# Flamingo-style gated decoder: layer 2's keys, queries and values of all batches projected in its setup and kept in DRAM scratch

## The reference

```python
x = x + tanh(g_xattn[0]) * L0_xattn(layernorm(x), ctx, ctx)     # layer 1
x = x + tanh(g_ffn[0])   * L0_ffn(layernorm(x), ...)
x = x + tanh(g_xattn[1]) * L1_xattn(layernorm(x), ctx, mask, ...)  # layer 2
x = x + tanh(g_ffn[1])   * L1_ffn(layernorm(x), W1, W2)

# L1_xattn: 16 heads of 32 columns
q = w8a8_linear(x, wq, bq)            # rows and weights rounded to whole numbers of 8 bits
k = cond @ wk.T + bk
v = cond @ wv.T + bv
attn = softmax(q @ k.T / sqrt(32) + mask)
return w8a8_linear(attn @ v, wo, bo)

# L1_ffn: W1 and W2 rounded to -1, 0, 1; rows rounded to whole numbers
return bitlinear(silu(bitlinear(x, W1)), W2)
```

## Time and profile before

| | us |
|---|---|
| median of 3 runs | 1078.93 |
| lowest, highest | 1077.7, 1079.21 |
| profiled execution | 1081.88 |
| its span in the profile | 1080.1 |

### The profile page before, as it was taken

One profiled execution on the slowest core, in us unless ns is written; L12 is line 12 of the kernel. 1 busy time (PEld: TensorE's weight loads), 2 busy tenths in 40 slices (PEclk: granted clock), 3 DMA queues, 4 the chain that ended last, 5 costly groups with the idle time before them and its releaser, 6 DMA issues.

```text
span 1080.1 us, 16123 instructions
## 1 busy us (share of the span) xinstructions
PE 938.5 (87%) x5776; PEld 621.2 (58%) x5784; DVE 743.1 (69%) x1925; ACT 555.1 (51%) x1104; POOL 72.6 (7%) x53
## 2 busy tenths in 40 slices
PE   3999879999999977569989889998989998899567
PEld 2777767767767654356644456644566544566333
DVE  5887863361626058479978688786699796799564
ACT  3444412221212137358854679845689647689243
POOL 4444100000000000000010000010000010000100
PEclk9999989999999998879999999999999999999869
DMA  6331400010203066861017820019420149300001
GB/s 214 117 117 39 156 1 1 32 48 1 78 1 117 1 214 237 192 156 41 2 39 157 195 78 2 4 53 208 128 79 2 40 86 197 108 2 2 1 0 40
DMA packets 45888, 85.99 MB, mean 80 GB/s; under 512 B 7409, under 2 KB 7409, under 8 KB 44785
## 3 DMA queue, kind: packets, MB, share of 16 engines
q1 hardware_dynamic: 42448, 80.24, 26.9%
q0 software_dynamic: 576, 4.19, 1.1%
q10 hardware_dynamic: 2784, 0.54, 0.3%
HBM read 43.01 MB, written 8.39 MB: 48 GB/s over the span
## 4 chain that ended last, share of the span: by engine, by line
PE 33%; DVE 10%; SPq 6%; issue 6%; DMA 5%; ACT 4%; POOL 0%; POOLq 0%; DVEq 0%; ACTq 0%
PE psum L1309 7%; PE psum L1326 6%; PE psum L1284 5%; PE psum L1382 5%; PE psum L1352 5%; SPq L962 5%; DMA k<-k_lo 4%; ACT probs L1110 2%; PE psum L1251 1%; PE psum L1368 1%; DVE amax L1531 1%; SPq L973 1%; DVE probsT L1619 1%; DVE xn L1699 1%; PE psum L1335 1%
## 5 line engine op out<-in xcount | busy, mean ns | idle before, releaser
L1110 ACT ACTIVATE probs<-psum,neg_max 128x512 f32<-128x512 f32 x256 | 174.8, 692 | 32.1 <-DVE neg_max L1593 32.0
L1593 DVE CUSTOM_DVE_ANT_0 psum<-psum,m_in 128x512 f32<-128x512 f32 x256 | 174.0, 702 | 18.5 <-issue 18.5
L1309 PE MATMUL psum<-ident,probs 128*128 128x128 f32 x1024 | 154.0, 274 | 0.0
L1309 PEld LDWEIGHTS psum<-ident,probs 128*128 128x128 f32 x1024 | 127.4, 141 | 21.0 <-issue 3.3
L1284 PE MATMUL psum<-k,q 128*128 128x512 f32 x256 | 125.9, 497 | 13.4 <-ACT probs L1110 8.3
L505 PE MATMUL psum<-w_sb,hT 128*128 128x512 f32 x256 | 115.1, 593 | 0.0
L389 ACT ACTIVATE hT<-psum,b_col 128x256 f32<-128x256 f32 x64 | 26.8, 470 | 136.2 <-PE psum L425 136.2
L1619 DVE COPY probsT<-psum 128x512 f32<-128x512 f32 x128 | 87.7, 685 | 2.6 <-PE psum L1309 2.3
L423 PE MATMUL psum<-xselT_hi,w_hi 128*128 128x256 f32 x256 | 82.8, 323 | 4.2 <-ACT onehotT L383 4.2
L1101 ACT COPY probsT<-psum 128x512 f32<-128x512 f32 x128 | 75.1, 587 | 19.8 <-PE psum L1309 19.8
L945 POOL TENSOR_TENSOR xres<-xres,xn 128x512 f32<-128x512 f32 x16 | 19.9, 1274 | 876.4 <-DVE xn L1699 876.4
(11 more groups left out here) (207 smaller groups left out, 1685.5 us busy)
## 6 DMA issues: line engine op xcount, KB each, us to landing
c_in<-in_ctx_dram SPq DMA_DIRECT2D x8, 1024.0 KB, 5.4
bw_in<-in_L_ffn_W_dram SPq DMA_DIRECT2D x8, 1024.0 KB, 11.2
k<-k_hi SPq DMA_DIRECT2D x32, 256.0 KB, 6.8
k<-k_lo SPq DMA_DIRECT2D x32, 256.0 KB, 8.5
q<-q_hi SPq DMA_DIRECT2D x64, 128.0 KB, 2.7
q<-q_lo SPq DMA_DIRECT2D x64, 128.0 KB, 2.4
xres<-in_x_dram SPq DMA_DIRECT2D x4, 1024.0 KB, 5.3
w_raw<-in_L_ffn_w_dram POOLq DMA_DIRECT2D x4, 1024.0 KB, 5.1
```

The lines of the kernel that those rows point to most:

```text
L1110: act.activation(probs[:, u % 4, :], psum[u % SCORE_BANKS][:, :], ACT.Exp, scale=-1.0, bias=neg_max[:, u:u + 1], accum_out=prob_sum[:, nt, ...
L1309: mm = pe.transpose(turn_bank(u)[:, l * P:(l + 1) * P], probs[:, u % 4, l * P:(l + 1) * P], ident[:, :])
L1593: dve.tensor_tensor_reduce(bank[:, :], bank[:, :], m_in[:, nt, :], -1.0, LOWEST, ALU.add, ALU.min, neg_max[:, u:u + 1]).then_inc(masked_re ...
```

## The change

Layer 2's setup makes the keys, queries and values of all four batches (`project`, on PE, ACT and DVE, with all three queues written so that batch b+1's context is turned between batch b's value tiles). SP writes them to DRAM scratch (`k_dram`, `q_dram`, `v_dram`) between its loads. The attention of batch b loads `k4`, `q4` (16 transfers of 256 KB each, into 32 partitions, four per group of four heads) and `vv` from there; group g of batch b+1 is loaded once batch b's scores of group g are made. The tails lose their projections.

Other parts of the edit:

- Keys and values: weights and context are split into a high half and the rest, and a product is three matmuls in a single pass each (`three`) instead of one in float32. DVE makes the low halves. Two banks serve the keys and two the values, so tile 2 waits for the eviction of tile 0.
- Both feed-forward weights pass through one input buffer `bw_in` in the place of `k4`; the first is turned in batch 1's projection and the second in batch 3's. ACT rounds all chunks, DVE clips them.
- The queries' rows of x are loaded into `xn` and worked on in place; `x_in` for batch 0 is the last of the initial loads.
- The value products of a half group are spread over four steps instead of two (`i % 2 == 0`).

```diff
+    k_dram = nc.dram_tensor("k_dram", (B, 2, C, S), F32, kind="Internal").ap()
+    q_dram = nc.dram_tensor("q_dram", (B, 2, C, S), F32, kind="Internal").ap()
+    v_dram = nc.dram_tensor("v_dram", (B, S, C), F32, kind="Internal").ap()
...
+        bw2T = at("bw2T", [P, FT, C], FP8, bw2T_at)
...
+        c_in = at("c_in2", [P, T, C], F32, x_at)
+        ctxT = [[at(f"ctxT{s}{i}", [P, CT_, S], F32R, q4_at + 16 * K * s + 8 * K * i) for i in range(2)] for s in range(2)]
+        k_hi = at("k_hi", [P, CT_, S], F32R, kst_at)
+        k_lo = at("k_lo", [P, CT_, S], F32R, kst_at + 8 * K)
+        q_hi = at("q_hi", [P, CT_, S], F32R, xres_at)
+        q_lo = at("q_lo", [P, CT_, S], F32R, probs_at)
+        q_raw = at("q_raw", [P, CT_, S], F32, probs_at)
+        v_out = [m_in, m_in, m_in, xn]
         BWC = FT * C // 4
-        bw_in = [at("bw_in0", [P, 4, BWC], F32, k4_at), at("bw_in1", [P, 4, BWC], F32, q4_at)]
-        bw_whole = [at(f"bw_whole{k}", [P, BWC], BF16, (xres_at, probs_at)[k // 2] + 4 * K * (k % 2)) for k in range(4)]
-        magnitudes = [at(f"magnitudes{k}", [P, BWC], BF16, m_at + 4 * K * k) for k in range(2)]
+        bw_in = at("bw_in", [P, 4, BWC], F32, k4_at)
...
+                def load_keys(b, g):
+                    for i, part in enumerate((0, 1, 0, 1)):
+                        sp.dma_start(k4[HD * i:HD * (i + 1), HPG * g:HPG * (g + 1), :].bitcast(F32),
+                                     k_dram[b, part, P * g:P * (g + 1), :].rearrange("(r d) s -> d r s", d=HD)
+                                     ).then_inc(k4_loaded[g], 16)
...
+                def save_keys(b):
                     sp.wait_ge(k_hi_ready, b * CT_ + CT_)
                     sp.wait_ge(k_lo_ready, b * CT_ + CT_)
-                    for g, part in enumerate((k_hi, k_lo, k_hi, k_lo)):
-                        for r in range(HPG):
-                            sp.dma_start(k4[HD * g:HD * (g + 1), r::HPG, :].bitcast(F32),
-                                         part[HD * r:HD * (r + 1), :, :].bitcast(F32)).then_inc(k_stacked, 16)
-
-                def stack_queries(b, q_hi, q_lo):
-
-                    for half in range(2):
-                        sp.wait_ge(q_hi_ready, b * CT_ + 2 * half + 2)
-                        sp.wait_ge(q_lo_ready, b * CT_ + 2 * half + 2)
-                        for g, part in enumerate((q_hi, q_hi, q_lo, q_lo)):
-                            for r in range(HPG):
-                                heads = slice(2 * half * HPG + r, 2 * (half + 1) * HPG, HPG)
-                                sp.dma_start(q4[HD * g:HD * (g + 1), heads, :].bitcast(F32),
-                                             part[HD * r:HD * (r + 1), 2 * half:2 * half + 2, :].bitcast(F32)
-                                             ).then_inc(q_stacked[half], 16)
-
+                    for i, part in enumerate((k_hi, k_lo)):
+                        sp.dma_start(k_dram[b, i].rearrange("(c p) s -> p c s", p=P),
+                                       part[:, :, :].bitcast(F32)).then_inc(k_saved, 16)
...
                 sp.wait_ge(sh.x2_stored, 16 * B)
-                sp.wait_ge(magnitude_ready, 7)
+                for b in range(B):
+                    if b + 1 < B:
+                        sp.wait_ge(qxT_psum, 2 * b + 2)
+                        load_rows(b + 1)
+                    save_keys(b)
+                    if b == 1:
+                        for k in range(4):
+                            sp.wait_ge(bwT_psum, 2 * k + 2)
+                            sp.dma_start(bw_in[:, k, :], bw2[P * k:P * (k + 1), :]).then_inc(bw_loaded[1][k], 16)
+                    save_queries(b)
+                    if b + 2 < B:
+                        sp.wait_ge(ctxT_psum, (b + 2) * CT_)
+                        load_context(b + 2)
+                    if b + 1 < B:
+                        save_values(b)
+                sp.wait_ge(v_saved, 3 * 16)
                 sp.dma_start(m_in[:, :, :], rows(mask, 0)).then_inc(m_loaded, 16)
...
+                sp.dma_start(vv[:, :, :], rows(v_dram, 0)).then_inc(vv_loaded, 16)
+                sp.wait_ge(k_saved, 32)
+                sp.wait_ge(q_saved, 32)
+                sp.wait_ge(bwT_psum, 16)
+                for g in range(GROUPS):
+                    load_keys(0, g)
+                    if g < 2:
+                        load_queries(0, g)
+                save_values(B - 1)
+                for g in range(2, GROUPS):
+                    load_queries(0, g)
+                sp.dma_start(x_in[:, :, :], rows(x_mid, 0)).then_inc(x_loaded, 16)
+
+                for b in range(B):
+                    if b + 1 < B:
+                        sp.wait_ge(x_used, b * T + T)
+                        sp.dma_start(x_in[:, :, :], rows(x_mid, b + 1)).then_inc(x_loaded, 16)
+                        for g in range(GROUPS):
+                            sp.wait_ge(score_psum, b * UNITS + GU * (g + 1))
+                            sp.wait_ge(k_saved, 32 * (b + 2))
+                            sp.wait_ge(q_saved, 32 * (b + 2))
+                            load_keys(b + 1, g)
+                            load_queries(b + 1, g)
+                        sp.wait_ge(masked_ready, (b + 1) * UNITS)
+                        sp.dma_start(m_in[:, :, :], rows(mask, b + 1)).then_inc(m_loaded, 16)
+                        sp.wait_ge(av_psum, (b + 1) * HG)
+                        sp.wait_ge(v_saved, 16 * (b + 2))
+                        sp.dma_start(vv[:, :, :], rows(v_dram, b + 1)).then_inc(vv_loaded, 16)
...
+                def project(b):
+                    normed_queries(b)
+                    key_highs(b, range(2))
+                    if b == 0:
+                        magnitude(0, 0)
+                    rounded_queries(b)
+                    key_highs(b, range(2, 3))
+                    query_scales(b)
+                    turned_rows(b, (2, 3))
+                    key_highs(b, range(3, CT_))
+                    if b % 2 == 0:
+                        for k in range(1 if b == 0 else 0, 4):
+                            magnitude(b // 2, k)
+                    query_highs(b)
+                    if b % 2:
+                        turned_bw(b // 2)
+                    if b + 1 < B:
+                        turned_context(b + 1, range(CT_))
+                    if b % 2 == 0:
+                        round_chunks(b // 2)
...
+                def three(dst, left, right, start, stop):
+
+                    (l_hi, l_lo), (r_hi, r_lo) = left, right
+                    pe.matmul(dst, l_hi, r_hi, start=start, stop=False)
+                    pe.matmul(dst, l_hi, r_lo, start=False, stop=False)
+                    return pe.matmul(dst, l_lo, r_hi, start=False, stop=stop)
...
+                def keys(b, tiles):
+                    for o in tiles:
+                        if o >= 2:
+                            pe.wait_ge(k_lo_ready, b * CT_ + o - 1)
+                        for c in range(CT_):
+                            if o == 0:
+                                pe.wait_ge(ctxT_lo_ready, b * CT_ + c + 1)
+                            mm = three(psum[o % 2][:, :], [p[:, c, o * P:(o + 1) * P] for p in wkT],
+                                       [p[:, c, :] for p in ctxT[b % 2]], c == 0, c == CT_ - 1)
+                        mm.then_inc(k_psum, 1)
+
+                def values(b, t):
+                    if t >= 2:
+                        pe.wait_ge(v_ready, b * T + t - 1)
+                    else:
+                        pe.wait_ge(q_scaled, b * CT_ + t + 1)
                     for c in range(CT_):
-                        for t in range(CT_):
-                            mm = pe.transpose(psum_b[4 * i + c][:, t * P:(t + 1) * P], w_whole[:, i, t, c * P:(c + 1) * P],
-                                              ident_b[:, :])
-                        mm.then_inc(linear_psum, 1)
-                for i, (w, ready) in enumerate(((wk_in, linear_act_ready), (wv_in, linear_dve_ready))):
+                        mm = three(psum[2 + t % 2][:, :], [p[:, c, t * P:(t + 1) * P] for p in ctxT[b % 2]],
+                                   [p[:, c, :] for p in wvT], c == 0, c == CT_ - 1)
+                    mm.then_inc(v_psum, 1)
...
+                def project(b):
+
+                    if b:
+                        pe.wait_ge(q_scaled, b * CT_)
+                    keys(b, range(3))
+                    query_rows(b)
+                    keys(b, range(3, CT_))
+                    queries(b)
+                    if b % 2:
+                        turn_bw(b // 2)
+                    for t in range(T):
+                        values(b, t)
+                        if b + 1 < B:
+                            context(b + 1, (t,))
+                    if b % 2 == 0:
+                        pe.wait_ge(sxrow_ready, b + 1)
+                        bw_sums(b // 2)
...
+                        if 0 <= hg < HG and i % 2 == 0:
+                            l = i // 2
...
+                pe.wait_ge(v_ready, B * T)
```

(31 more changed lines are left out.)

## The result

The kernel after takes 1192.75 us (median of 4 runs, 1191.26 to 1194.8), the kernel before 1078.32 beside it. The ratio is 1.1067, 95% interval 1.1038 to 1.1095: slower, 5.8 us above the forecast 1187 and inside its range. The profiled execution has a span of 1192.7 us, 112.6 more than before.

What follows compares the result with a forecast made beforehand. PE was busy 87% of the span, attention bound by a mix of DVE, ACT and PE. First score +130.4, x_in +25.5, batches -39.7, value products -8.0: +108.2 on 1081.9, 1190.1, less 3.0 to the median: 1187, range 1125 to 1225.

Steps and rivals of the forecast that it cites:

- first score: Layer 2's setup: with four projections ahead of it, PE's first attention score moves from 471.2 to 601.6 us, +130.4.
- stall for x_in: Batch 0's ninth attention step: DVE waits for x_in, last in SP's load queue, landing at 637 but due at 611.5, +25.5.
- batches: Tails of three batches lose their projections, each worth 13.2 us by comparing batch 0 with batch 3: -39.7 us.
- value products: Attention: spreading them over four steps instead of two uses DVE's gap per half group; 8 us gained taken.
- The bound below: Attention: low end of the gain allowed for spreading value products, between 0 and 22 us.
- R0: Setup: moment DVE finishes the root for batch 0, put at 413.8 us, 24.7 after the setup's start.
- even batches: Setup: from DVE's finished root in an even batch to the next batch's root, 39.7 us.
- the odd one: Setup: from DVE's finished root in batch 1 to the next, with weight rounding and turning, 56 us.
- last R to first score: End of setup: from DVE's finished root for batch 3 (R3, 549.2) to the first score (601.6), 52.4 us.
- rival C: Setup: PE sets the pace, values end at 539.5 and the first score comes at 547; 1133 us, chance 0.15.
- Rival D: Setup: further waits of the same kind, say 8 us in each projection, +32; 1219 us, chance 0.20.
- Rival E: Batch tails: next attention could run into the tail, so batches gain far more, deciding from 3 x 49 us; chance 0.01.

Runs made afterwards that it cites:

- x_in early: Kernel after, with only SP's load of batch 0's x_in moved to when the last context is turned, not behind k4 and q4: 1172.63 us.
- without projections: Kernel before, with batches 1 to 3 making no context, keys, values, queries or stacking and scoring against batch 0's: 1036.73 us.
- one product: Kernel after, with each keys and values product in layer 2 one matmul (high half by high half) instead of three: 1171.76 us.
- the query highs: Kernel after, with ACT making the queries' high halves ahead of the magnitudes in batches 0 and 2: 1189.31 us.
- the rounding: Kernel after, with ACT's rounding of the feed-forward weight chunks moved into gaps in batches 1 and 3: 1186.42 us.
- the turned banks: Kernel after, with DVE turning the weight banks before making the query low halves in batches 1 and 3: 1194.38 us.
- Three mended: Kernel after with x_in early, query highs first, rounding later, plus batch 0's group 0 of q4 and k4 loaded ahead of its values: 1158.11 us.

## Why the prediction was right, and where it was off

The terms of the sum, in us:

| term | predicted | measured |
|---|---|---|
| first score | +130.4 | +129.3 |
| stall for x_in | +25.5 | +23.3 to the residual; 21.8 taken back by x_in early |
| batches | -39.7 | -40.0, and -41.1 without projections |
| value products | -8.0 | 0 |
| sum | +108.2 | +112.6 |

**The step that failed** is "The value products are spread over four steps of a half group instead of two", worth 8. I took DVE's gap for the room to gain. But the earlier trace rows had PE busy 8.44 of 8.75 us, more than DVE: moving PE's work about inside a stretch that PE fills can't shorten it, whatever DVE could do. The bound below, nothing, was the right end: the spread measured 0 us in both kernels. Without this term the sum would have been 116.2 and the forecast 1195.

**The first score.** Its 130.4 was right in part because errors cancelled. Layer 1, whose code is the same, ended 4.1 us earlier in this execution, so the setup was 133.4 us longer and not 129.3. From its start to the first score I had 212.5 us and it took 215.5. The pieces: R0 24.7 after the start (measured 23.6), even batches 39.7 (42.9 and 41.8), the odd one 56 (53.8), last R to first score 52.4 (53.3). How near the first of these comes depends on the execution: it was 39.8 where the granted clock was 1.00. PE's idle before key tile 2 was predicted as 6 and 12 us and was 5.5 in batch 2 and 10.8 in the odd batches. In batch 0 it did not appear: PE starts its keys after R there, so PE and the evictions go hand in hand.

**The queues set the pace, not the sums.** PE is busy 138.2 of 191.9 us, so rival C, which has PE busy throughout, fails; one product shows the same from the other side, with 58 us of work gone and 23.9 gained. Rival D's further 8 us in each projection did not come: the setup was 3.0 us longer than laid out. But no single wait is the cause: taking the query highs, the rounding or the turned banks out of the way gave 3.4, 6.3 and 0 us, the last because a gain in batch 1 was lost again before the first score. Three mended together, x_in with its 20.1 among them and group 0 moved forward, gave 1192.75 - 1158.11 = 34.6.

**The stall.** Its place and cause were right. It was 21.5 us (DVE's own wait) and not 25.5: x_in was due at 612.2 instead of 611.5, and was there at 633.7 instead of 637, as the loads into 32 partitions went at 221 to 226 GB/s and not 208. The other 1.8 us to the residual lie in the first steps, where PE's granted clock was 0.50 (window 600 to 608, above); that the clock is their cause was not tested.

**The batches.** Reading the worth of the projections from batch 3, whose tail has none, gave 39.7; the profiles of two kernels give 40.0 and 41.1, and the times of the second 40.4. Rival E's 3 x 49 is out. In the setup a period is 191.9 / 4 = 48.0 us, with PE busy for 34.5 of them. Part of that is the feed-forward weights, which the setup before had as well. Like for like, the setup had one projection and has four, and grew by 133.4 us: 44.5 for each of the three. This is the whole result: what cost 13.2 us beside the LayerNorm chain costs 44.5 by itself.

What stays open: why the granted clock of the same code differs between executions, which moves the first period by some 4 us, and what group 0 ahead of the values is worth by itself.

## What to carry to other kernels

Before work is moved out of a busy-looking stretch, price it there by a stretch that already lacks it, not by its busy time: here a projection was worth 13.2 us in the tail and lengthened the setup by 44.5, where there was no chain of other work for it to hide behind. And whatever one moves to the front of an in-order DMA queue, look at what is last in it and when its reader is due: here one MiB cost 20 us.

## What the hardware showed that was not expected

Identical code of layer 1 started layer 2's setup at 382.9 to 389.1 us in different executions; in the kernel before its granted clock was 0.94 and 0.92 in two stretches where the kernel after had 1.00 and 0.95. The first projection's period, again of the same code, was 39.8 us at a clock of 1.00, 42.9 at 0.92 and 43.9 at 0.88. So a term of a few us read from one profile has that much in it that isn't the change's. Read against the wrong one of them, the first period would have credited the query highs with 4.0 us instead of 0.8.

Loads from DRAM into 32 partitions ran at 221 to 226 GB/s, SBUF to SBUF stacking at 208, and the same loads over 128 partitions at 404 to 406, all with DMA engines that the view calls fully busy: the busy share doesn't tell a slow destination from a fast one.
